# Second graph layer: scores of own frames only, Exp behind the transposes, the routing's tables a step earlier, separate roots

## The chip, the cores and the metric

The kernel runs on one core of one Trainium2 chip. The metric is the device time of one execution in microseconds (us), smaller is better. A measurement of this kernel consists of several runs.

## What is computed

The reference is a stack of two layers over 128 frames of 64 nodes with 128 channels each; a layer is a graph part and a feed-forward part with experts, each added to its input. The change touches the graph part of the second layer and the routing that follows it:

```
def _L1_gnn_ref(inp, adj, W1, W2, W3):
    h1, h2, h3 = inp @ W1, inp @ W2, inp @ W3            # per node
    e = leaky_relu(h1 . h2 within the frame, 0.2)         # 64 x 64 per frame
    e = where(adj > 0, e, NEG_INF)
    return relu(softmax(e) @ h3)
x = x + _L1_gnn_ref(_layernorm(x), adj, W1, W2, W3)
x = x + _L1_ffn_ref(_layernorm(x), Wg, bg, W1, b1, W2, b2)   # top 2 of 8 experts by x @ Wg + bg
```

The second line's experts are computed in a last stage. Before it each token's normalized row has to be written twice into lists in DRAM, one list for each expert, at a position that a running count gives.

## The kernel before, in words

Four phases follow one another: the first graph layer with attention and routing, the first experts, the second graph layer with its routing (`phase_gnn1`, L2357 on), and the last experts (`phase_last`, L2762 on). Only `phase_gnn1` and its class `SplitRouting` (L1230 on) change. All names below are of these two.

The tokens lie in SBUF as 64 pairs of frames: 128 partitions are the 2 x 64 nodes of a pair. Four pairs are a group, and 16 groups are worked on one after another in a software pipeline that is written out by hand: `in_pairs` calls each engine's own `step(g, ...)` for g = -3 to 20, and inside it each piece names the group it works on. Engines meet by semaphores: `x.now(i)` waits for the piece of group i, `x.before(i)` for that of the group in front.

The pieces of a group, in the order in which its data pass them:
- `head_x` on DVE (L2354) adds the first experts' two rows to x; `head_stats` (L280 to L286) takes mean and variance; `roots` on POOL (L2720) takes the reciprocal root by a power; `head_xn` on DVE (L2629) normalizes.
- `head_T` on PE (L2450) transposes the four pairs, ScalarE (ACT) copies them out (L2541), `head_h` (L2458, L2459, L2462) forms h1, h2 and h3, and ACT copies these (L2545, L2552).
- `scores` on PE (L2472, L2475) writes the mask and adds h1 . h2 for whole pairs, 128 x 128 each, of which the two 64 x 64 blocks on the diagonal are used. `scores_own` on ACT (L2572) copies the two blocks out, `soft` on DVE (L2638 to L2645) applies the leaky slope, takes the row maximum and subtracts it. `exp` on ACT (L2581) writes the exponentials into `pr`, whose other blocks were set to zero once (L2418).
- `probs_T` on PE (L2484) transposes `pr`, ACT copies (L2588), `mix` on PE (L2496) multiplies 128 rows of the transposed probabilities with h3 and a column of ones, `norm` on DVE (L2655) takes the reciprocal of the sums, `mixed_out` on ACT (L2563) scales and clips, `residual` on DVE (L2662) adds to x.
- For the routing, `flat_stats` (L280 to L286) and the same `roots` instruction on POOL give a second normalizing, `flat_norm` (L2676) writes the rows, `flat_T` on PE (L2507) transposes them, ACT copies (L2595), `logits` on PE (L1269) multiplies with the routing's matrix.
- Batches of eight pairs (the first two and the last two have four) are then routed: `vector_choose` on DVE (L1304 to L1332) finds the two best experts, `tensor_rank` on PE (L1283, L1286) counts, `vector_rows` on DVE (L1348 to L1357) turns counts into row positions, and `pool_scatter` (L1384) has POOL issue two indirect DMAs for each pair, 128 in all. At most three are under way (`OUT`): each waits for the landing of the third one before it. Position tiles and the three `flat` tiles are used again once their scatters have landed.

The order of the steps is what the change rewrites. Before, in step g the routing's normalizing, transposes and logits belong to group g - 1, and a batch is chosen when `batch_due(g, 3)` holds, that is two steps after its last group. One `roots` instruction in each step serves the head of group g + 2 and the routing of group g - 1. POOL issues up to 16 scatters of a batch in three parts (6, 8 and 2) over three steps, each part behind that step's `roots`:

```
2723                def step(g, b, h):
2724                    roots(g)
2725                    t, u, v = [batch_due(g, lag) for lag in (3, 4, 5)]
```

SP's queue fetches the first experts' rows (L2345, as `head_x` frees a buffer), loads the last stage's weights (L2743) and stores x (L2739). After the last batch's positions DVE builds the last stage's tables (L1443 on), SP writes padding rows behind each list (L1484), waits for the last scatters, and gathers the first rows (L1507).

Of the kernel before, what the change touches and what calls it, by code (L numbers as in the profile page):

```python
# [21 lines left out]
PG = 4  # L22
# [1207 lines left out]
class SplitRouting:  # L1230
# [3 lines left out]
    def __init__(self, ctx, nc, name, consts, base, bias):  # L1234
# [16 lines left out]
        self.pos = [sb(f"pos{i}", [128, 2, PB], I32) for i in range(2)]  # L1251
# [89 lines left out]
    def vector_rows(self, dve, t, bank):  # L1341
# [14 lines left out]
        self.wait_landed(dve, t - 2)  # L1356
        dve.tensor_copy(self.pos[t % 2][:, :, 0:n], self.posf[:, :, 0:n]).then_inc(s.sem, 1)  # L1357
# [16 lines left out]
    def pool_scatter(self, pool, t, first, last, flat, dest):  # L1374
# [4 lines left out]
        for n in range(first, last):  # L1379
# [4 lines left out]
            pool.indirect_dma_start(out=dest, out_offset=bass.IndirectOffsetOnAxis(ap=self.pos[t % 2][:, k, p:p + 1], axis=0),  # L1384
# [972 lines left out]
def phase_gnn1(nc, W, x, banks, c, T, rows1, dest, ahead, wall, out_dram, resident, tile_w):  # L2357
# [3 lines left out]
    with ExitStack() as ctx:  # L2361
# [8 lines left out]
        st, mv = sb("st", [128, 2, PG, 6]), sb("mv", [128, 2, PG, 2])  # L2370
# [9 lines left out]
        pr = sb("pr", [128, PG, 2, NODES])  # L2380
        pt = sb("pt", [128, PG, 128])
# [20 lines left out]
        xT_ready, h12_ready, p_ready, pt_ready, fT_ready = sig("xT_ready"), sig("h12_ready", 2), sig("p_ready", 2), sig("pt_ready"), sig("fT_ready")  # L2402
        own_ready = sig("own_ready", 2)
        act_signals = [xT_ready, h12_ready, h3_ready, own_ready, p_ready, pt_ready, o_ready, fT_ready] + R.act_signals
        root_ready = sig("root_ready")
        pool_signals = [root_ready] + R.pool_signals
# [4 lines left out]
        def own(f):  # L2411

            return bE[64 * f:64 * f + 64, :].rearrange("n (p f m) -> n p f m", p=PG, f=2)[:, :, f, :]

        with nc.Block() as block:
            @block.gpsimd
            def _(pool):
                pool.memset(pr[:, :, :, :], 0.0).then_inc(setup, 1)  # L2418
                pool.memset(h3[:, :, C:C + 1], 1.0).then_inc(setup, 1)
                open_signals(pool, pool_signals)  # L2420
# [20 lines left out]
        with nc.Block() as block:  # L2441
            @block.tensor
            def _(pe):
                def head_T(i):
                    if not runs(i):
                        return
                    pe.wait_ge(*fT_ready.before(i, turns=3))
# [5 lines left out]
                def head_h(i):  # L2453
# [7 lines left out]
                    for p in range(PG):  # L2461
                        ins = pe.matmul(bH3[:, 128 * p:128 * p + 128], xT[:, 128 * p:128 * p + 128], w3[:, :],  # L2462
                                        start=(p == 0), stop=True, skip_group_check=True)
                    ins.then_inc(pe_h.sem, 1)

                def scores(i):
                    if not runs(i):
                        return
                    pe.wait_ge(*pt_ready.before(i))
# [607 lines left out]
```

## Time and profile before

| what | value |
|---|---|
| median of 3 runs | 1493.25 us (1490.9 to 1496.06) |
| span of the profiled execution | 1492.9 us |
| time of the profiled execution outside the span | none is given |
| busy: PE, DVE, ACT, POOL | 79%, 69%, 50%, 58% of the span |
| phase of the change, from the page's slices and the timeline | some 912 to 1197 us |

The span is that of one execution under the profiler; the runs are timed without it. A line of a view names engine, line of the kernel, operation, what is written from what with shapes, and a count; a time in brackets is the engine's idle time before it and what ended it. PE is TensorE's products, PEld its weight loads, DVE VectorE, ACT ScalarE, POOL GpSimd, and SP the engine that issues most DMAs. The granted clock is given as a share of TensorE's full clock.

### The profile page before, as it was taken

To read this page: it belongs to the slowest core of one execution; us is meant where nothing else is said; L and a number is where in the kernel's file an instruction comes from. 1 tells how busy PE (TensorE), PEld (TensorE's weight loads), DVE (VectorE), ACT (ScalarE), POOL (GpSimd) and SP (SyncE) were. 2 spreads that over 40 slices of the span, in tenths; PEclk is the share of its full clock that TensorE was granted. 3 is DMA by queue.
4 is the path that set the end of the run, shared out by engine and by line. 5 is a ranking of instruction groups with operands and counts; after the bars stand their busy time and mean duration, and the time that the engine had idled before them with its cause. 6 is when DMAs were issued, how large, how long until landed. Compare 5 with 4: busy or idle time off the path is not lost. (4 is left out here: it accounts for less than half of the span.)

```text
span 1492.9 us, 32014 instructions
## 1 busy us (share of the span) xinstructions
PE 1180.9 (79%) x8595; PEld 1004.2 (67%) x8595; DVE 1029.2 (69%) x3960; ACT 742.6 (50%) x1864; POOL 869.1 (58%) x742
## 2 busy tenths in 40 slices
PE   5888888767888772599999994666775089999996
PEld 3666656557878772488888883545554079989995
DVE  3788888999888874367777765667775435565554
ACT  5777777546676772133333331434443035555553
POOL 3466666552556777344444442245776748887887
PEclk9999999979898995799999997879777579999999
DMA  7300000000000111466666664233421225545553
GB/s 188 54 2 2 2 1 2 2 1 1 30 30 32 39 41 57 141 196 196 196 196 196 196 209 138 84 93 92 122 94 60 78 50 72 71 63 71 71 69 45
DMA packets 126249, 122.53 MB, mean 82 GB/s; under 512 B 16576, under 2 KB 108096, under 8 KB 126128
## 3 DMA queue, kind: packets, MB, share of 16 engines
q1 hardware_dynamic: 92720, 85.65, 20.4%
q0 software_dynamic: 32960, 35.36, 12.0%
q8 instruction: 53, 0.87, 0.3%
q14 instruction: 68, 0.56, 0.1%
q10 hardware_dynamic: 448, 0.10, 0.0%
HBM read 76.71 MB, written 44.34 MB: 81 GB/s over the span
## 5 line engine op out<-in xcount | busy, mean ns | idle before, releaser
L2866 POOL DMA_INDIRECT out<-m_yb,m_dsti x142 | 228.4, 1608 | 64.3 <-DVE m_yb L2966 26.9
L2160 POOL DMA_INDIRECT rows<-m_yb,m_dsti x135 | 129.2, 957 | 169.5 <-DVE m_dsti L2291 147.9
L1384 POOL DMA_INDIRECT dispatch<-g_flat,g1r_pos x128 | 129.4, 1011 | 76.0 <-issue 32.3
L2236 ACT ACTIVATE m_sg<-psum 128x256 f32<-128x256 f32 (+3 forms) x216 | 79.8, 370 | 178.7 <-PE psum L2189 174.8
L1126 POOL DMA_INDIRECT dispatch<-common_v,a1r_pos x128 | 129.3, 1010 | 54.3 <-issue 35.5
L2939 ACT ACTIVATE m_hT<-psum,m_w 128x256 f32<-128x256 f32 (+1 forms) x240 | 92.8, 447 | 100.7 <-PE psum L2893 99.8
L2189 PE MATMUL psum<-m_xT,m_w 128*128 128x256 f32 (+3 forms) x648 | 140.3, 366 | 0.7 <-ACT m_xT L2227 0.7
L2189 PEld LDWEIGHTS psum<-m_xT,m_w 128*128 128x128 f32 (+1 forms) x648 | 106.2, 178 | 18.3 <-ACT m_xT L2227 0.9
L2904 PE MATMUL psum<-m_w,m_hT 128*128 128x128 f32 x848 | 104.7, 275 | 3.1 <-DVE m_yb L2962 3.1
L2893 PE MATMUL psum<-m_xT,m_w 128*128 128x256 f32 (+1 forms) x480 | 104.9, 363 | 1.0 <-issue 0.8
L2904 PEld LDWEIGHTS psum<-m_w,m_hT 128*128 128x128 f32 x848 | 99.4, 192 | 3.7 <-issue 2.8
L2272 DVE TENSOR_TENSOR m_hT<-psum,m_sg 128x256 f32<-128x256 f32 (+3 forms) x216 | 80.1, 402 | 20.6 <-ACT m_sg L2236 18.9
L2893 PEld LDWEIGHTS psum<-m_xT,m_w 128*128 128x128 f32 x480 | 81.8, 195 | 9.7 <-issue 2.0
L2199 PE MATMUL psum<-m_w,m_hT 128*128 128x128 f32 (+1 forms) x606 | 76.6, 274 | 0.5 <-DVE m_yb L2256 0.5
L491 PE MATMUL psum<-ident,common_s 128*128 128x128 f32 x256 | 41.6, 285 | 42.0 <-ACT common_s L635 42.0
L2199 PEld LDWEIGHTS psum<-m_w,m_hT 128*128 128x128 f32 (+1 forms) x606 | 71.9, 191 | 0.8 <-DVE m_hT L2272 0.7
L2759 DVE COPY m_w<-resident 128x1156 f32 x60 | 47.6, 793 | 35.4 <-issue 35.3
L2033 POOL TENSOR_TENSOR a_root<-a_pin,a_cube 128x12 f32<-128x12 f32 (+2 forms) x20 | 38.8, 1941 | 54.1 <-DVE a_pin L1987 50.8
L491 PEld LDWEIGHTS psum<-ident,common_s 128*128 128x128 f32 x256 | 27.9, 142 | 61.0 <-ACT common_s L635 60.8
L2256 DVE TENSOR_TENSOR m_yb<-psum,m_share 128x256 f32<-128x256 f32 (+1 forms) x72 | 29.4, 408 | 56.6 <-PE psum L2199 49.7
L480 PE MATMUL psum<-g_k,g_q 128*128 128x256 f32 x256 | 65.7, 379 | 0.0
L720 DVE TENSOR_REDUCE g_mx<-psum 128x8 f32<-128x512 f32 x64 | 43.9, 686 | 23.4 <-PE psum L480 23.4
(316 smaller groups left out, 3219.4 us busy)
## 6 DMA issues: line engine op xcount, KB each, us to landing
m_w<-in_c_wall SPq DMA_DIRECT2D x54, 533.0 KB
ahead_w<-in_c_wall SPq DMA_DIRECT2D x18, 533.0 KB, 4.2
g1c_y<-rows SPq DMA_DIRECT2D x32, 256.0 KB, 3.4
m_xg<-dispatch SPq DMA_DIRECT2D x47, 132.0 KB
m_xg<-dispatch SPq DMA_DIRECT2D x46, 130.0 KB, 2.2
resident<-in_c_wall SPq DMA_DIRECT2D x8, 578.0 KB, 6.0
out<-x SPq DMA_DIRECT2D x16, 256.0 KB, 5.9
out<-m_yb,m_dsti POOLq DMA_INDIRECT x142, 3.3
```

What stands on the lines that cost most here:

```text
L491: ins = pe.transpose(bPT[:, 128 * hp:128 * hp + 128], s[:, p % 2, 2 * hp:2 * hp + 2, :].rearrange("p h m -> p (h m)"), ident[:, :])
L1126: pool.indirect_dma_start(out=dest, out_offset=bass.IndirectOffsetOnAxis(ap=self.pos[t % 2][:, k, p:p + 1], axis=0), in_=flat[:, p, :], in ...
L1384: pool.indirect_dma_start(out=dest, out_offset=bass.IndirectOffsetOnAxis(ap=self.pos[t % 2][:, k, p:p + 1], axis=0), in_=flat[:, p, :], in ...
L2160: pool.indirect_dma_start(out=rows_out, out_offset=bass.IndirectOffsetOnAxis(ap=dsti[j][:, t:t + 1], axis=0), in_=yb[j][:, t, :], in_offse ...
L2189: i = pe.matmul(bank[0:cn, TILE * m:TILE * m + rows], w[j][:, HID * m + c0:HID * m + c0 + cn], xT[j % 2][:, 0:rows], start=(m == 0), stop= ...
L2199: i = pe.matmul(bY[:, 128 * t:128 * t + 128], hT[jj % 2][0:cn, k, 128 * t:128 * t + 128], w[jj][0:cn, W2 + 128 * k:W2 + 128 * k + 128], st ...
L2236: act.activation(sg[j % 2][0:cn, k, 0:rows], up_banks[j % 2][k][0:cn, 0:rows], ACT.Silu)\
L2272: dve.tensor_tensor(hT[j % 2][0:cn, k, 0:rows], up_banks[j % 2][k][0:cn, TILE:TILE + rows], sg[j % 2][0:cn, k, 0:rows], ALU.mult).then_inc ...
L2866: pool.indirect_dma_start(out=out_rows, out_offset=bass.IndirectOffsetOnAxis(ap=dsti[j][:, t:t + 1], axis=0), in_=yb[j][:, t, :], in_offse ...
L2893: i = pe.matmul(bank[0:cn, TILE * (k % 2):TILE * (k % 2) + rows], w[j][:, c0:c0 + cn], xT[j % 2][:, 0:rows], start=(k % 2 == 0), stop=True ...
L2904: i = pe.matmul(bY[:, 128 * t:128 * t + 128], hT[jj % 2][0:cn, k, 128 * t:128 * t + 128], w[jj][0:cn, HID + 128 * k:HID + 128 * k + 128], ...
L2939: act.activation(hT[j % 2][0:cn, n, 0:rows], bank[0:cn, TILE * (n % 2):TILE * (n % 2) + rows], ACT.Gelu, bias=w[j][:, b1:b1 + 1]).then_inc ...
```

## The change

- Scores: only the blocks of own frames are formed, 64 x 64 each, into one half of a bank (`own`); the mask covers 256 columns in place of 512. ACT copies them once with the factor 0.2, and DVE takes the maximum of that copy and of `own` itself.
- The shifted scores `s` are transposed as two blocks of 128 x 128 (`turned`, the other half of the bank) and Exp is applied when ACT copies the result into `pt`. `pr`, its memset, `exp` and `p_ready` go.
- `mix` works on 64 rows and 64 columns at a time: eight products in place of four, whose input rows and output partitions take either half of the array. h3 is formed in eight products, so that its rows lie where these need them.
- Order: each engine's step g now begins with the transposes of the shifted scores of group g, which the step before has made, and ends with `flat_norm`, `flat_T` and `logits` of group g itself. A batch is chosen when `batch_due(g, 2)` holds, one step after its last group. `scores` and `soft` are those of group g + 1.
- `roots` becomes `root_head(g + 2)` and `root_flat(g)`, each an instruction of its own on four columns, with scatters between them. A batch's 16 scatters come in parts of 3, 4, 4 and 5.
- A third position tile; `mv` is split, with two tiles for the heads.

The core of the diff:

```diff
-        self.pos = [sb(f"pos{i}", [128, 2, PB], I32) for i in range(2)]
+        self.pos = [sb(f"pos{i}", [128, 2, PB], I32) for i in range(3)]
...
-        self.wait_landed(dve, t - 2)
-        dve.tensor_copy(self.pos[t % 2][:, :, 0:n], self.posf[:, :, 0:n]).then_inc(s.sem, 1)
+        self.wait_landed(dve, t - 3)
+        dve.tensor_copy(self.pos[t % 3][:, :, 0:n], self.posf[:, :, 0:n]).then_inc(s.sem, 1)
...
-        def own(f):
-
-            return bE[64 * f:64 * f + 64, :].rearrange("n (p f m) -> n p f m", p=PG, f=2)[:, :, f, :]
+        own, turned = bE[:, 0:256], bE[:, 256:512]
...
+                    for f in range(2):
+                        for p in range(PG):
+                            r, n = 64 * (p % 2), 2 * (p // 2) + f
+                            ins = pe.matmul(bH3[r:r + 64, 128 * n:128 * n + 128], xT[:, 128 * p + 64 * f:128 * p + 64 * f + 64], w3[:, :],
+                                            start=(f == 0 and p < 2), stop=True, skip_group_check=True)
+                    ins.then_inc(pe_h.sem, 1)
...
+                    pe.wait_ge(*e_steps.before(i, 0))
+                    pe.wait_ge(*h12_ready.now(i, 1))
+                    mk = bass.AP(mask, 0, [mask[:, :].ap[0], [0, PG], [1, NODES]])
+                    pe.matmul(own, identb[:, :], mk, start=True, stop=False, skip_group_check=True)
                     for p in range(PG):
-                        ins = pe.matmul(bH3[:, 128 * p:128 * p + 128], xT[:, 128 * p:128 * p + 128], w3[:, :],
-                                        start=(p == 0), stop=True, skip_group_check=True)
-                    ins.then_inc(pe_h.sem, 1)
-
-                def scores(i):
+                        for f in range(2):
+                            t = slice(128 * p + 64 * f, 128 * p + 64 * f + 64)
+                            ins = pe.matmul(own[64 * f:64 * f + 64, 64 * p:64 * p + 64], h1[:, t], h2[:, t], start=False, stop=True,
+                                            skip_group_check=True)
+                    ins.then_inc(pe_e.sem, 1)
...
-                    pe.wait_ge(*h12_ready.now(i, 1))
-                    mk = bass.AP(mask, 0, [mask[:, :].ap[0], [0, 2 * PG], [1, NODES]])
-                    pe.matmul(bE[:, :], identb[:, :], mk, start=True, stop=False, skip_group_check=True)
-                    for p in range(PG):
-                        t = slice(128 * p, 128 * p + 128)
-                        ins = pe.matmul(bE[:, t], h1[:, t], h2[:, t], start=False, stop=True, skip_group_check=True)
-                    ins.then_inc(pe_e.sem, 1)
-
...
-                    pe.wait_ge(*p_ready.now(i, 1))
-                    for p in range(PG):
-                        ins = pe.transpose(bE[:, 128 * p:128 * p + 128], pr[:, p, :, :].rearrange("n f m -> n (f m)"), ident[:, :])
+                    pe.wait_ge(*e_steps.now(i, 2))
+                    for q in range(2):
+                        ins = pe.transpose(turned[:, 128 * q:128 * q + 128], s[:, 2 * q:2 * q + 2, :].rearrange("n p m -> n (p m)"), ident[:, :])
...
-                    for u, bank in enumerate([bO0, bO1]):
-                        for n in range(2):
-                            p = 2 * u + n
-                            ins = pe.matmul(bank[:, (C + 1) * n:(C + 1) * n + C + 1], pt[:, p, :], h3[:, p, :],
-                                            start=(n == 0), stop=True, skip_group_check=True)
-                        ins.then_inc(pe_o.sem, 1)
+                    for u in range(2):
+                        for n, bank in enumerate([bO0, bO1]):
+                            for f in range(2):
+                                r = slice(64 * n, 64 * n + 64)
+                                ins = pe.matmul(bank[64 * f:64 * f + 64, (C + 1) * u:(C + 1) * u + C + 1], pt[r, u, 64 * f:64 * f + 64],
+                                                h3[r, 2 * u + f, :], start=(u == 0), stop=True, skip_group_check=True)
+                            if u == 1:
+                                ins.then_inc(pe_o.sem, 1)
...
                 def step(g, b, h):
-                    scores(g)
+                    probs_T(g)
                     head_T(g + 1)
+                    mix(g)
                     head_h(g + 1)
-                    probs_T(g)
-                    if b % 2 == 1:
-                        mix(g)
-                    t = batch_due(g, 3)
+                    scores(g + 1)
+                    t = batch_due(g, 2)
                     if t is not None:
                         R.tensor_rank(pe, t, bR)
-                    flat_T(g - 1)
-                    if b % 2 == 0:
-                        mix(g)
-                    logits(g - 1)
+                    flat_T(g)
+                    logits(g)
...
-                    for f in range(2):
-                        r = slice(64 * f, 64 * f + 64)
-                        act.activation(e0[r, :, :], own(f), ACT.Copy).then_inc(own_ready.sem, 1)
...
-                    for f in range(2):
-                        r = slice(64 * f, 64 * f + 64)
-                        act.activation(pr[r, :, f, :], s[r, :, :], ACT.Exp).then_inc(p_ready.sem, 1)
+                    act.activation(e0[:, :, :].rearrange("n p m -> n (p m)"), own, ACT.Copy, scale=0.2).then_inc(own_ready.sem, 1)
...
-                    act.activation(pt[:, :, :].rearrange("m p n -> m (p n)"), bE[:, :], ACT.Copy).then_inc(pt_ready.sem, 1)
+                    act.activation(pt[:, :, :].rearrange("m q n -> m (q n)"), turned, ACT.Exp).then_inc(pt_ready.sem, 1)
...
                 def step(g, b, h):
-                    scores_own(g)
+                    probs_T(g)
+                    head_xT(g + 1)
+                    mixed_out(g)
                     head(g + 1)
-                    exp(g)
-                    probs_T(g)
-                    t = batch_due(g, 3)
+                    scores_own(g + 1)
+                    head_h3(g + 1)
+                    t = batch_due(g, 2)
                     if t is not None:
                         R.scalar_exp(act, t, batch_rows(flat, t))
-                    flat_T(g - 1)
-                    mixed_out(g)
-                    head_h3(g + 1)
+                    flat_T(g)
...
-                    dve.wait_ge(*own_ready.now(i, 1))
+                    dve.wait_ge(*own_ready.now(i))
                     dve.wait_ge(*e_steps.before(i))
-                    dve.scalar_tensor_tensor(out=e1[:, :, :], in0=e0[:, :, :], scalar=0.2, in1=e0[:, :, :],
-                                             op0=ALU.mult, op1=ALU.max).then_inc(e_steps.sem, 1)
+                    dve.tensor_tensor(e1[:, :, :], own.rearrange("n (p m) -> n p m", p=PG), e0[:, :, :], ALU.max).then_inc(e_steps.sem, 1)
...
-                               vs[1], i, EPS_LN, gate, [x3_ready.now(i)] + ([root_ready.now(i + 2)] if i > 0 else []))
+                    norm_stats(dve, lambda p: xt(i, p), st[:, 1, :, :], mv1, ve[:, 1, :], bn[1], part[1],
+                               vs[1], i, EPS_LN, gate, [x3_ready.now(i), rs1_ready.before(i)])
...
-                    dve.wait_ge(*root_ready.now(i + 3))
+                    dve.wait_ge(*rs1_ready.now(i))
...
                 def step(g, b, h):
-                    flat_stats(g - 1)
-                    soft(g)
-                    t = batch_due(g, 3)
+                    t = batch_due(g, 2)
+                    norm(g)
+                    head_x(g + 3, 1 - b % 2)
                     if t is not None:
                         R.vector_choose(dve, t, bR)
-                    if b % 2 == 1:
-                        flat_norm(g - 1, h)
-                        norm(g)
-                        if t is not None:
-                            R.vector_rows(dve, t, bR)
-                        head_x(g + 3, 1 - b % 2)
-                        head_xn(g + 2)
                     else:
-                        if t is not None:
-                            R.vector_rows(dve, t, bR)
-                        head_x(g + 3, 1 - b % 2)
-                        flat_norm(g - 1, h - 1)
-                        head_xn(g + 2)
-                        norm(g)
-                    head_stats(g + 3)
+                        head_stats(g + 3)
                     residual(g)
+                    flat_stats(g)
+                    soft(g + 1)
+                    if t is not None:
+                        R.vector_rows(dve, t, bR)
+                    head_xn(g + 2)
+                    flat_norm(g, h)
+                    if t is not None:
+                        head_stats(g + 3)
...
-                def roots(g):
...
-                    pool.tensor_tensor(rs[:, lo:hi, :], ve[:, lo:hi, :], half[:, 0:PB].rearrange("t (k p) -> t k p", k=2)[:, lo:hi, :],
-                                       ALU.pow).then_inc(root_ready.sem, 1)
+                def root_head(i):
+                    if not runs(i):
+                        return
+                    pool.wait_ge(*vs[0].now(i))
+                    pool.wait_ge(*xn_ready.before(i))
+                    pool.tensor_tensor(rs[:, 0, :], ve[:, 0, :], half[:, 0:PG], ALU.pow).then_inc(rs0_ready.sem, 1)
...
+                def root_flat(i):
+                    if not runs(i):
+                        return
+                    pool.wait_ge(*vs[1].now(i))
+                    pool.wait_ge(*flat_ready.before(i))
+                    pool.tensor_tensor(rs[:, 1, :], ve[:, 1, :], half[:, 0:PG], ALU.pow).then_inc(rs1_ready.sem, 1)
...
+                def some(t, first, last):
+                    if t is not None and BATCHES[t][1] == PB:
+                        R.pool_scatter(pool, t, first, last, batch_rows(flat, t), dest)
 
                 def step(g, b, h):
-                    roots(g)
-                    t, u, v = [batch_due(g, lag) for lag in (3, 4, 5)]
-                    if v is not None and BATCHES[v][1] == PB and v < LAST_BATCH - 2:
-                        R.pool_scatter(pool, v, 14, 16, batch_rows(flat, v), dest)
-                    if u is not None and BATCHES[u][1] == PB:
-                        R.pool_scatter(pool, u, FIRST_PART if u == LAST_BATCH - 2 else 6, 14 if u < LAST_BATCH - 2 else 16, batch_rows(flat, u), dest)
-                    if t is not None:
-                                R.pool_scatter(pool, t, 0, 2 * PG if BATCHES[t][1] == PG else FIRST_PART if t == LAST_BATCH - 2 else 6, batch_rows(flat, t), dest)
+                    t, u, v = [batch_due(g, lag) for lag in (2, 3, 4)]
+                    root_head(g + 2)
+                    if v != LAST_BATCH - 2:
+                        some(v, 11, 16)
+                    some(u, 3, 7)
+                    root_flat(g)
+                    some(u, 7, 11 if u != LAST_BATCH - 2 else 16)
+                    some(t, 0, 3)
+                    if t is not None and BATCHES[t][1] == PG:
+                        R.pool_scatter(pool, t, 0, 2 * PG, batch_rows(flat, t), dest)
```

## Rows read from the trace of the kernel before

**Rows 1.** One line's instructions, L1384: ns min/median/max, first and last start in us.
```profile
L1384 POOL DMA_INDIRECT dispatch<-g_flat,g1r_pos x128: 952/958/1485, 963.1 to 1194.0; - x128
```

**Rows 2.** Groups of POOL by line and shape, 912 to 1197 us: busy, mean ns, idle before.
```profile
L1384 POOL DMA_INDIRECT dispatch<-g_flat,g1r_pos x128 | 129.4, 1011 | 76.0 <-issue 32.3 <-DVE g1r_pos L1357 26.4 <-DMA dispatch<-g_flat,g1r_pos 17.0
...
L2720 POOL TENSOR_TENSOR g_rs<-g_ve,half 128x4 f32<-128x4 f32 x6 | 6.9, 1154 | 14.3 <-DVE g_ve L286 14.2
```

**Rows 3.** Timeline (start us, us, engine, line): last positions, first gather of the last stage.
```profile
1174.85 0.17 DVE L1357 CAST g1r_pos<-g1r_posf 128x8 int32<-128x8 f32 x1 [6.20 <-DMA dispatch<-g_flat,g1r_pos]
...
1196.55 0.41 SPq L1507 DMA_DIRECT2D ahead_xg<-dispatch  x1
```

**Rows 4.** Timeline of DVE, one choosing and one unbroken run, 1006 to 1021 us.
```profile
1006.06 0.21 DVE L1304 TENSOR_TENSOR g1r_lg<-psum,W_bg 128x64 f32<-128x64 f32 x1
...
1009.11 1.11 DVE L2676 TENSOR_SCALAR g_flat<-x,g_mv,g_rs 128x128 f32<-128x128 f32 x4
...
1011.87 0.31 DVE L1348 TENSOR_TENSOR g1r_rows<-psum,stab_base 128x144 f32<-128x144 f32 x1 [0.16 <-PE psum L1286]
...
1013.02 1.41 DVE L2354 TENSOR_TENSOR x<-x,g1c_y 128x512 f32<-128x512 f32 x2
...
1014.35 1.11 DVE L2629 TENSOR_SCALAR g_xn<-x,g_mv,g_rs 128x128 f32<-128x128 f32 x4
...
1015.37 0.86 DVE L280 BATCH_NORM_STATS2 g_st<-x 128x6 f32<-128x128 f32 x4
...
1016.87 0.68 DVE L2662 TENSOR_TENSOR x<-x,g_o 128x512 f32<-128x512 f32 x1
...
1020.51 1.44 DVE L2354 TENSOR_TENSOR x<-x,g1c_y 128x512 f32<-128x512 f32 x2
```

**Rows 5.** Busy time by stretch: sum of PE, PEld, DVE, ACT, POOL, then granted clock.
```profile
1005.00:1024.00 19.00, 11.71 (x74) 8.40 (x74) 14.50 (x58) 9.31 (x22) 9.67 (x8) 1.00 0.21 62
...
1069.00:1079.00 10.00, 8.54 (x29) 6.13 (x29) 8.89 (x34) 4.07 (x10) 7.59 (x8) 0.50 0.32 99
```

**Rows 6.** Timeline, PE and DVE, at the lower clock.
```profile
1068.78 1.09 PE L2507 MATMUL psum<-ident,g_flat 128*128 128x128 f32 x4 [3.78 <-DVE g_flat L2676]
...
1072.27 0.59 PE L2472 MATMUL psum<-g_mask,identb 128*128 128x512 bf16 x1
...
1145.92 1.09 PE L2484 MATMUL psum<-ident,g_pr 128*128 128x128 f32 x4 [3.22 <-ACT g_pr L2581]
...
1147.74 2.06 PE L2496 MATMUL psum<-g_h,g_pt 128*128 128x129 f32 x8 [0.73 <-issue]
...
1149.84 0.17 DVE L2655 RECIPROCAL g_rc<-psum 128x2 f32<-128x2 f32 x1 [0.69 <-PE psum L2496]
```

**Rows 7.** Timeline of PE at the upper clock.
```profile
1010.37 1.13 PE L2496 MATMUL psum<-g_h,g_pt 128*128 128x129 f32 x8 [0.73 <-issue]
...
1011.69 0.64 PE L2507 MATMUL psum<-ident,g_flat 128*128 128x128 f32 x4
...
1013.92 0.38 PE L2472 MATMUL psum<-g_mask,identb 128*128 128x512 bf16 x1
```

**Rows 8.** Timeline of PE, two more transposes after a wait.
```profile
964.70 1.08 PE L2507 MATMUL psum<-ident,g_flat 128*128 128x128 f32 x4 [3.57 <-DVE g_flat L2676]
...
1136.92 0.63 PE L2507 MATMUL psum<-ident,g_flat 128*128 128x128 f32 x4 [3.13 <-DVE g_flat L2676]
```

**Rows 9.** Timeline of PE and PEld in the first layer, 200 to 212 us.
```profile
201.69 1.08 PE L453 MATMUL psum<-g_xT,g_wqkv 128*64 128x256 f32 x8
...
208.16 1.03 PE L480 MATMUL psum<-g_k,g_q 128*128 128x256 f32 x4
...
201.69 0.63 PEld L453 LDWEIGHTS psum<-g_xT,g_wqkv 128*64 128x64 f32 x8 [0.17 <-issue]
```

**Rows 10.** Timeline, first scores and the load of Exp's table.
```profile
930.33 1.05 PE L2475 MATMUL psum<-g_h 128*128 128x128 f32 x8
...
935.58 1.28 ACT L2581 ACT_TABLE_LOAD   x1
```

More of the change, by code:

```diff
@@ L2369, in phase_gnn1 @@
         mask = sb("mask", [128, NODES], BF16)
-        st, mv = sb("st", [128, 2, PG, 6]), sb("mv", [128, 2, PG, 2])
+        st = sb("st", [128, 2, PG, 6])
+        mv0, mv1 = [sb(f"mv0{i}", [128, PG, 2]) for i in range(2)], sb("mv1", [128, PG, 2])
         ve, rs = sb("ve", [128, 2, PG]), sb("rs", [128, 2, PG])
@@ L2379, in phase_gnn1 @@
         s = sb("s", [128, PG, NODES])
[L2380 to L2381 removed]
+        pt = sb("pt", [128, 2, 128])
         rc = sb("rc", [128, PG])
@@ L2446, in head_T @@
                         return
-                    pe.wait_ge(*fT_ready.before(i, turns=3))
+                    pe.wait_ge(*fT_ready.before(i, turns=2))
                     pe.wait_ge(*xn_ready.now(i, PG - 1))
@@ L2502, in flat_T @@
                         return
-                    if runs(i + 2):
-                        pe.wait_ge(*xT_ready.now(i + 2))
+                    if runs(i + 1):
+                        pe.wait_ge(*xT_ready.now(i + 1))
                     pe.wait_ge(*flat_ready.now(i, PG - 1))
@@ L2535, in _, with head_xT @@
             def _(act):
-                def head(i):
+                def head_xT(i):
                     if not runs(i):
@@ L2541, in head @@
                     act.activation(xT[:, :], bT[:, :], ACT.Copy).then_inc(xT_ready.sem, 1)
+                def head(i):
+                    if not runs(i):
+                        return
                     for n, (bank, h) in enumerate([(bH1, h1), (bH2, h2)]):
@@ L2556, in mixed_out @@
                         return
-                    for u, bank in enumerate([bO0, bO1]):
-                        act.wait_ge(*rc_ready.now(i, u))
+                    for n, bank in enumerate([bO0, bO1]):
+                        act.wait_ge(*rc_ready.now(i, n))
                         act.wait_ge(*x3_ready.before(i))
                         ov = bank[:, 0:2 * (C + 1)].rearrange("n (p c) -> n p c", p=2)
-                        for n in range(2):
-                            p = 2 * u + n
-                            act.activation(o[:, p, :], ov[:, n, 0:C], ACT.Relu, scale=rc[:, p:p + 1]).then_inc(o_ready.sem, 1)
+                        for u in range(2):
+                            act.activation(o[:, 2 * u + n, :], ov[:, u, 0:C], ACT.Relu, scale=rc[:, 2 * n + u:2 * n + u + 1]).then_inc(o_ready.sem, 1)
                 def scores_own(i):
@@ L2619, in head_stats @@
                         return
-                    norm_stats(dve, lambda p: xt(i, p), st[:, 0, :, :], mv[:, 0, :, :], ve[:, 0, :], bn[0], part[0],
-                               vs[0], i, EPS_LN, gate, [M.mixed.now(i, 1), root_ready.before(i)])
+                    norm_stats(dve, lambda p: xt(i, p), st[:, 0, :, :], mv0[i % 2], ve[:, 0, :], bn[0], part[0],
+                               vs[0], i, EPS_LN, gate, [M.mixed.now(i, 1), rs0_ready.before(i)])
                 def head_xn(i):
@@ L2642, in soft @@
                     dve.wait_ge(*e_steps.now(i, 1))
-                    dve.wait_ge(*p_ready.before(i))
+                    dve.wait_ge(*pe_pt.before(i))
                     m = mx[:, :]
```

37 lines of the change are left out of this document (11 added, 26 removed).

## Prediction

> **What bounds the kernel now.** I first read the page's 40 slices to find the stage that the change touches: the second graph layer with its routing lies between the two expert stages. Then I listed all instructions of GpSimd (POOL) in it. Its 128 scatters start between 963.1 and 1194.0 us [rows 1], each takes 0.96 us, and some 0.30 us of issue (32.3 us over 109) lies before the next [rows 1, 2]; so one costs 1.26 us of POOL. The last ends at 1194.96 us, and 1.6 us later SP gathers the first rows of the last stage [rows 3]. That stage works through a fixed list of tiles, so the whole kernel ends later or sooner by what this gather moves. 128 scatters are 161 us of a stretch of 232 us; the rest are roots, waits for positions (26.4 us) and waits for landings (17.0 us) [rows 2]. So POOL ends the stage, with one batch of work after another, and the question is when the last batches reach it. Next I read the timeline of VectorE (DVE) for the price of every piece of a step [rows 4], and that of TensorE at its two clock levels [rows 5 to 8].
>
> **The new loop.** Afterwards a step on DVE begins with the reciprocals of group g, which wait for the mixing products, and ends with the normalizing into the routing's rows, on which the transposes of the same group wait. Those are followed on TensorE, in its queue's order, by the logits, by the transposes of the next group's scores and by its mixing, and only then DVE has work again (but for a statistics piece in routing steps). No step can overlap the next there. A step is therefore DVE's pieces plus one **turn** through TensorE and ScalarE, which I call L.
>
> DVE's pieces, from start to start [rows 4]: routing's rows 1.15 us (1011.87 to 1013.02), adding the experts' rows 1.33, normalizing for the next head 1.02, first statistics 1.50 (1015.37 to 1016.87), residual with second statistics and softmax 3.64 (to 1020.51), choosing 3.05 (1006.06 to 1009.11), normalizing for the routing 1.11, and 0.17 for the second reciprocal. A plain step holds 0.17 + 1.33 + 1.50 + 3.64 + 1.02 + 1.11 = 8.77 us. A routing step has choosing and rows in addition, and its statistics go behind the last piece, into the turn: 11.47 us. The half batches I take as full ones; that is some tenths too much.
>
> The turn at the lower clock: flat's transposes to the instruction behind the logits 3.49 us (1068.78 to 1072.27); the scores' transposes to the second reciprocal 3.92 us (1145.92 to 1149.84) [rows 6]. From the latter goes about 0.4, since two transposes of the four remain (their 1.09 us is at most halved), and about 0.2 for an Exp over 256 columns where a copy over 512 stood; I take 0.4 us for that Exp, and leave the mixing as it is. Added is 0.17 us of idle weight load where full blocks give way to half ones [rows 9], once on this path. Sum 7.0 us. At the upper level the first part is 2.23 us (1011.69 to 1013.92), and the second loses 2.06 - 1.13 = 0.93 of mixing and 0.23 of transposes [rows 6, 7]: 2.2 + 2.1 + 0.2 = 4.5 us.
>
> **The mixing blocks.** Four products of 128 rows become eight of 64 by 64. Upper bound among likely prices: two half-wide blocks share the array, so the mixing costs what it costs now. The trace shows just that for column halves: eight instructions of 128 by 64 over 256 columns took 1.08 us, four of full width 1.03 [rows 9]. Lower bound: blocks that differ in rows share it too, and the mixing is halved, which takes 1.0 us from the turn at the lower clock and 0.55 at the upper (6.0 and 4.0 us). No row reaches that; I take the middle, 6.5 and 4.25 us; the two ends are rivals below.
>
> **The clock.** The granted clock was 1.00 from 1005 to 1024 us and 0.50 from 1069 to 1079 us, its two levels of 2.4 and 1.2 GHz [rows 5]. Four transposes take 0.63 us at the one and 1.09 at the other. Of four resumptions after TensorE had waited between 3.1 and 3.8 us, three were at the lower level (964.70, 1068.78, 1145.92) and one at the upper (1136.92) [rows 6, 8]. Afterwards TensorE has nothing to do from the end of the scores to flat's transposes, while DVE does most of its pieces, that is for a good part of its 8.8 to 11.5 us in each step, and so at least as long as in those four waits. So I take the lower level for three turns in four: L = 0.75 x 6.5 + 0.25 x 4.25 = 5.9 us.
>
> **The sum.** The first scores come as now (930.33 us [rows 10]), then 0.7 for them, 0.4 for the copy, 1.2 for the softmax, 0.5 for two transposes, 1.28 for the load of Exp's table [rows 10], 0.4 for Exp, 1.2 for mixing: step 0 begins at 936 us. Before step 14 lie seven plain and seven routing steps: 7 x 8.77 + 7 x 11.47 = 141.7, less 2.8 us at group 13, which has no more head to add and measure. Step 14 starts at 1074.9 + 14 L. It has 9.1 us on DVE (11.47 less 1.33 and 1.02), so step 15 starts at 1084.0 + 15 L. Its second statistics are done after 0.17 + 3.05 + 2.4 = 5.6 us. The root for them stands in POOL's queue ahead of 25 scatters (nine of batch 7, eight each of 8 and 9): 0.2 + 1.15 for the root [rows 2] and 25 x 1.26 = 31.5 us. The last scatter ends at 1122.5 + 15 L = 1211 us. Now it is 1195.0, so the stage ends 16 us later. Break-even is L = 4.83 us.
>
> What lies beside this: SP's path from the last positions to the gather is 21.7 us now (1174.85 to 1196.55 [rows 3]); afterwards step 15's pieces (7.9) end at 1084 + 88.5 + 7.9 = 1180.4, the first part of a turn, choosing, counting and rows (3.5 + 3.05 + 0.5 + 1.15) bring the positions at 1188.6, and the gather could go at 1210, 2 us ahead of the scatters' landing. The third position buffer removes the 6.20 us wait of that row; without it POOL would still end last. Narrower scores, one copy of own blocks in place of two, and third products in half blocks cost and save nothing, as DVE's pieces cover them; without that cover they are worth under 1 us in a step. Single roots (32 for 19) need 1.15 us each on POOL [rows 2], which has 16 x 1.26 + 4 x 1.4 = 25.8 us of work in a pair of steps of 8.77 + 11.47 + 2 L = 32 us; so POOL idles in mid-stage, and its landing waits (17.0 us in all now) mostly vanish in that room. DMAs and SP's queue keep their number and order. Routing a step sooner brings the first scatter to 936 + 8.77 + 5.9 + 9.3 = 960 us, 3 us sooner than 963.1: the longer steps in front take back what the shift gives.
>
> The profiled execution spans 1492.9 us, 0.35 below the median of the runs shown, 1493.25; no time outside the span is given. 1492.9 + 16 = **1509 us**.
>
> **Rivals.**
> - Faster: TensorE keeps its upper level through the turns. For it speaks the resumption at 1136.92 [rows 8]; against it, the three others. Then L is 4.0 to 4.5, the last scatter ends at 1182.5 to 1190, and the time is 1480 to 1488 us. It decides as soon as L falls below 4.83.
> - No change: some 70 turns in 100 at the upper level, L from 4.55 to 5.1, 1488.4 to 1497.4 us.
> - Four blocks share the array: L = 0.75 x 6.0 + 0.25 x 4.0 = 5.5, the end at 1205, 1503 us. Only pairs share it: L = 0.75 x 7.0 + 0.25 x 4.5 = 6.4, 1516 us. The Trainium skill (TensorEngine Tiling (Array Packing), Tiling Modes) has four 64x64 tiles work independently; by that rule it is the former. The same section says that changing the tiling mode drains the engine, which speaks against this change; the trace agrees with a small price, the 0.17 us of rows 9.
> - Much slower: half blocks run one at a time, the mixing doubles, and L is about 8.2: 1543 us. Rows 9 speak against it, for columns at least. Further waits (own scores late for the softmax, a root behind scatters that wait for landings) would stop on the way there.
> - The earlier routing does what it says and POOL, started sooner, ends the stage sooner. For that POOL would have to be the bound throughout, and its 25.8 us in a pair of steps against at least 20.2 + 2 x 4.0 speak against it. That the routing hardly starts sooner at all (the 3 us above) is part of every case here.
>
> **How the numbers follow.** A measurement of this kernel can tell about 0.3%, 4.5 us. The forecast with L from 5.2 to 7.1 (1498 to 1527 us) gets 0.61; in it, 0.25 are for sharing by four, 0.20 for pairs alone, 0.16 between them. The much slower rivals get 0.10, the faster one 0.15, no change 0.14. So slower is 0.71. The forecast's own range is 1498 to 1527. The range for all, 1486 to 1527, takes in no change and the upper edge of the faster rival, and leaves out some 0.1 on each side.
>
> **What would show it.** DVE should idle before its reciprocals, waiting for the mixing, by some 4 to 7 us in each of 16 steps. Between 930 and 1170 us the granted clock should be lower than 0.8. Pairs of steps should last about 32 us; under 29.7 the forecast of the sign is wrong. POOL's wait for the second statistics should replace its waits for positions, and the last scatter should end near 1211 us. The mixing's group shows whether four blocks share the array. If flat's transposes resume at 0.63 us in most steps, my clock is wrong; if DVE's pieces overlap the turn, my loop is.

## The result and the profile after

The changed kernel took 1527.35 us (median of 4 runs, 1523.85 to 1527.66) against 1494.24 us before (4 runs, 1490.9 to 1496.06): 1.0221 times as long, 95% interval 1.0203 to 1.0239. It is slower, as forecast, but by 33 us where 16 were forecast, and 1527.35 lies 0.35 us above the range.

The profiled execution after spans 1525.7 us; its run took 1527.64 us, so 1.9 us lie outside the span. These are the scatters' line and the groups of POOL from 925 to 1240 us, which answer to [rows 1, 2]:

```profile
L1384 POOL DMA_INDIRECT dispatch<-g_flat,g1r_pos x128: 954/958/1442, 967.6 to 1228.7; - x128
...
L1384 POOL DMA_INDIRECT dispatch<-g_flat,g1r_pos x128 | 128.4, 1003 | 53.6 <-issue 35.6 <-DVE g1r_pos L1357 17.6 <-DVE g1r_posf L1354 0.3
L2700 POOL TENSOR_TENSOR g_rs<-g_ve,half 128x4 f32<-128x4 f32 x16 | 17.3, 1079 | 25.8 <-DVE g_xn L2621 16.7 <-DVE g_ve L286 8.9
L2707 POOL TENSOR_TENSOR g_rs<-g_ve,half 128x4 f32<-128x4 f32 x16 | 16.5, 1030 | 72.9 <-DVE g_ve L286 72.9
```

The first scatter went 4.5 us later than before and the last 34.7 us later. No scatter waits for a landing any more (17.0 us before), the waits for positions fell from 26.4 to 17.6 us, and POOL now stands 72.9 us in front of its second roots, waiting for DVE's statistics: POOL idles in mid-stage. The waits of DVE and PE from 925 to 1230 us (total, times, longest, in us) and the busy times from 930 to 1170 us, with the granted clock behind them, show for whom:

```profile
DVE g_rc L2646 <- PE psum L2498: 84.1, 16, 6.3
...
PE psum L2510 <- DVE g_flat L2667: 84.4, 16, 6.8
```

```profile
930.00:1170.00 240.00, 151.19 (x1078) 100.19 (x1078) 140.84 (x607) 71.59 (x174) 120.81 (x119) 0.70 0.28 83
```

DVE waits for the mixing and PE for DVE's rows, 84 us each, 16 times, in turn: DVE's pieces and the way through PE and ACT don't overlap, but for the statistics in routing steps. The granted clock is 0.70; it was 0.79 in the same stretch before. One whole turn, as the prediction calls that way, at the end of a routing step, in the timeline:

```profile
1054.65 0.87 DVE L280 BATCH_NORM_STATS2 g_st<-x 128x6 f32<-128x128 f32 x4
1054.88 1.09 PE L2510 MATMUL psum<-ident,g_flat 128*128 128x128 f32 x4 [6.40 <-DVE g_flat L2667]
...
1056.01 0.60 ACT L2587 ACTIVATE g_fT<-psum 128x512 f32<-128x512 f32 x1 [6.84 <-PE psum L2510]
...
1056.66 1.87 PE L1269 MATMUL psum<-W_wg,g_fT 128*128 128x8 f32 x8 [0.69 <-ACT g_fT L2587]
...
1058.38 0.67 PE L2485 MATMUL psum<-ident,g_s 128*128 128x128 f32 x2
...
1059.09 0.38 ACT L2580 ACTIVATE g_pt<-psum 128x256 f32<-128x256 f32 x1 [2.48 <-PE psum L2485]
...
1059.83 1.14 PE L2498 MATMUL psum<-g_h,g_pt 64*64 64x129 f32 x16
...
1061.01 0.26 DVE L2646 RECIPROCAL g_rc<-psum 128x2 f32<-128x2 f32 x2 [4.76 <-PE psum L2498]
```

From the end of the routing's normalizing (1053.88 + 0.85 = 1054.73) to the reciprocals is 6.27 us. In a routing step 1.5 us of it hold the statistics, and 4.76 us are idle; in a plain step all 6.27 are. The end of the stage, which answers to [rows 3]:

```profile
1205.35 0.22 DVE L1357 CAST g1r_pos<-g1r_posf 128x8 int32<-128x8 f32 x1
...
1228.66 0.96 POOL L1384 DMA_INDIRECT dispatch<-g_flat,g1r_pos  x1 [0.30 <-issue]
...
1231.25 0.41 SPq L1507 DMA_DIRECT2D ahead_xg<-dispatch  x1
```

The gather goes 34.7 us later than in [rows 3]. The experts' last rows before the stage were already 3.1 us later in this execution (909.6 against 906.5 us), in code that the change doesn't touch, and the last stage was 1.9 us shorter. So the stage itself is 31.6 us longer.

### The profile page after: what moved, and what is told of

Read it like the earlier page. It is cut to its first block and busy times, and to the rows that moved or that the text cites. A ratio compares the mean times of both kernels' runs of the same rounds, so it can differ in the third digit from the quotient of the medians.

```text
span 1525.7 us, 32671 instructions
## 1 busy us (share of the span) xinstructions
PE 1191.4 (78%) x8947; PEld 995.9 (65%) x8947; DVE 1026.1 (67%) x3960; ACT 719.5 (47%) x1816; POOL 872.2 (57%) x754
## 5 line engine op out<-in xcount | busy, mean ns | idle before, releaser
L1384 POOL DMA_INDIRECT dispatch<-g_flat,g1r_pos x128 | 128.4, 1003 | 53.6 <-issue 35.6
L2510 PE MATMUL psum<-ident,g_flat 128*128 128x128 f32 x64 | 15.9, 398 | 84.4 <-DVE g_flat L2667 84.4
L491 PE MATMUL psum<-ident,common_s 128*128 128x128 f32 x256 | 41.6, 286 | 41.8 <-ACT common_s L635 41.8
L491 PEld LDWEIGHTS psum<-ident,common_s 128*128 128x128 f32 x256 | 27.9, 142 | 60.8 <-ACT common_s L635 60.6
L2510 PEld LDWEIGHTS psum<-ident,g_flat 128*128 128x128 f32 x64 | 10.5, 201 | 85.8 <-issue 81.2
```

Source lines behind the costliest of these rows:

```text
L491: ins = pe.transpose(bPT[:, 128 * hp:128 * hp + 128], s[:, p % 2, 2 * hp:2 * hp + 2, :].rearrange("p h m -> p (h m)"), ident[:, :])
```

## The experiments

Seven kernels, compared with the kernel before on the same chip. In the profiles of all of them the experts' last rows start between 906.9 and 914.8 us, so stages are compared from that row on: to the gather it takes 290.0 us before and 321.6 us after.

**The new blocks in the old order.** The kernel before, with the scores', transposes', Exp's, mixing's and third products' pieces of the changed kernel and nothing else:

```diff
-                    act.activation(pt[:, :, :].rearrange("m p n -> m (p n)"), bE[:, :], ACT.Copy).then_inc(pt_ready.sem, 1)
+                    act.activation(pt[:, :, :].rearrange("m q n -> m (q n)"), turned, ACT.Exp).then_inc(pt_ready.sem, 1)
...
                     head(g + 1)
-                    exp(g)
                     probs_T(g)
```

> The change's blocks alone (own-frame scores, one copy, two wide transposes and then Exp, 64-row mixing and third products), in the order of work of the kernel before, with its joint roots, its routing three steps behind and its two position buffers. Theory (the new order costs the time, the blocks save a little): PE and ACT have less to do, POOL still ends the stage; last scatter between 1180 and 1196 us where it was 1194.0, time 1478 to 1497 us. Rival (half-size products, their changes of shape and the Exp behind the transposes cost it): 1505 to 1527 us.

Measured: 1486.58 us (8 runs), 0.9919 of before (0.9896 to 0.9941). The scatters' line of it:

```profile
L1384 POOL DMA_INDIRECT dispatch<-g_flat,g1r_pos x128: 956/962/1484, 960.9 to 1185.6; - x128
...
  issue: 40.1, 109
  DMA dispatch<-g_flat,g1r_pos: 17.7, 10
  DVE g1r_pos L1357: 11.4, 7
```

The blocks save 0.8%. With 1.0221 for the whole change, the rest of it (the order, with its single roots, scatter parts and third position tile; from here on "the order") costs 1.0221 / 0.9919 = 1.030, some 45 us. The stage takes 279.1 us, 42.5 less than in the changed kernel. Positions come sooner (11.4 us of waits for them, 26.4 before), which fits the shorter work on PE and ACT, and POOL's last scatter still ends the stage. The granted clock is hardly higher than in the changed kernel (0.71 from 930 to 1170 us, against 0.70): a low clock alone doesn't make the stage long.

**Flat's transposes and logits behind the next mixing.** The changed kernel with these on PE and ACT a step later, and routing with them:

```diff
-                    t = batch_due(g, 2)
+                    t = batch_due(g, 3)
...
-                    flat_T(g)
-                    logits(g)
+                    flat_T(g - 1)
+                    logits(g - 1)
```

> The changed kernel, with flat's transposes and logits of group g moved on PE and ACT behind the mixing of group g + 1, and routing a step later with them (three steps behind, as in the kernel before). Blocks, separate roots, DVE's order and three position buffers stay. Theory (a step is long because flat's transposes and logits stand between DVE's last piece and the next mixing): DVE's idle before the reciprocals falls from 4.8 to 6.3 us to under 4 us a step, a pair of steps from 33.0 to about 27 us; the later routing gives back one step of 13 us at the start; time 1470 to 1495 us. Rival (PE's and DVE's work itself is longer, or POOL is the bound): 1515 to 1535 us.

Measured: 1494.03 us (10 runs), 0.9976 of before (0.995 to 1.0002). Of the order's 45 us, (1.0221 - 0.9976) x 1494 = 37 are gone, and the stage takes 284.3 us, 37.3 less than in the changed kernel. DVE's reciprocals of a pair of steps show it, and what ends the pairs now:

```profile
1053.97 0.28 DVE L2646 RECIPROCAL g_rc<-psum 128x2 f32<-128x2 f32 x2
...
1056.86 0.87 DVE L280 BATCH_NORM_STATS2 g_st<-x 128x6 f32<-128x128 f32 x4 [1.30 <-POOL g_rs L2700]
...
1065.95 1.28 DVE L2667 TENSOR_SCALAR g_flat<-x,g_mv,g_rs 128x128 f32<-128x128 f32 x4 [2.83 <-POOL g_rs L2707]
1066.98 0.25 DVE L2646 RECIPROCAL g_rc<-psum 128x2 f32<-128x2 f32 x2
...
1079.79 1.28 DVE L2667 TENSOR_SCALAR g_flat<-x,g_mv,g_rs 128x128 f32<-128x128 f32 x4 [2.26 <-POOL g_rs L2707]
...
1082.33 0.28 DVE L2646 RECIPROCAL g_rc<-psum 128x2 f32<-128x2 f32 x2
```

The pair lasts 28.4 us (33.0 in the changed kernel), and its reciprocals wait for nothing; in the whole stage they wait 5.5 us where it was 84.1. In place of the mixing DVE waits for POOL's roots, 41.6 us in the stage (11.1 of them at once, for a head's root in step 4), and POOL has landing waits again (16.3 us). So the turn is off the path, and the waits now point to POOL; the last experiment tests that. The 8 us of the order that remain are not divided further: no kernel here has the new order with joint roots.

**Idle transposes in TensorE's wait.** The changed kernel with:

```diff
+WARM = (22, 36)
...
+                    for _ in range(WARM[batch_due(i, 2) is not None]):
+                        pe.transpose(bT[:, 0:128], ident[:, :], ident[:, :])
                     pe.wait_ge(*flat_ready.now(i, PG - 1))
```

> The changed kernel, with idle transposes of the identity (22 in a plain step, 36 in a routing step, into the bank that flat's transposes then overwrite) put into TensorE's wait for the normalized rows. Theory (the turn is 6.26 us because TensorE resumes at 1.2 GHz after its wait): the granted clock between 930 and 1170 us rises from 0.70 to over 0.9, the turn falls to 4.0 to 4.4 us, 16 turns give 30 to 36 us, time 1490 to 1498 us. Rival (what TensorE does in that wait doesn't set the clock of the turn): the idle transposes at 0.27 us each end after the rows are ready, by 1.8 us in a plain and 3.4 us in a routing step, and the time is 1550 to 1570 us.

Measured: 1508.17 us (10 runs), 1.0067 of before (1.0033 to 1.0101). The stage takes 304.0 us, 17.6 less than in the changed kernel, by the ratios it is 23 us less: between the theory and the rival. The granted clock from 930 to 1170 us rose to 0.82, not over 0.9. Idle transposes and the turn behind them, in TensorE's timeline:

```profile
1043.69 4.13 PE L2510 MATMUL psum<-ident 128*128 128x128 f32 x36
...
1049.38 0.66 PE L2513 MATMUL psum<-ident,g_flat 128*128 128x128 f32 x4 [1.57 <-DVE g_flat L2670]
1050.72 1.12 PE L1270 MATMUL psum<-W_wg,g_fT 128*128 128x8 f32 x8 [0.69 <-ACT g_fT L2590]
1051.69 0.67 PE L2486 MATMUL psum<-ident,g_s 128*128 128x128 f32 x2
...
1053.14 1.14 PE L2499 MATMUL psum<-g_h,g_pt 64*64 64x129 f32 x16
```

Flat's transposes now ran at the upper level in 14 turns of 16 (0.60 to 0.66 us). But the clock fell again inside the turn: here the logits took 1.12 us, near the 1.06 of the upper level (1.87 at the lower), but the scores' transposes and the mixing took the 0.67 and 1.14 us of the lower one. Only two of the 15 mixings behind a turn kept the upper level's 0.67 us from end to end. A turn wholly at the upper level, before the reciprocals at 1037.89 us, left DVE idle for 3.94 us, against 6.27 at the lower. So the clock does make the turn longer, and filling the wait in front of it isn't enough to hold it.

**Flat's transposes three times over.**

```diff
-                    for p in range(PG):
+                    for p in list(range(PG)) * 3:
```

> The changed kernel, with flat's four transposes done three times over into the same places: eight transposes more in each turn, 0.27 us each at the lower clock. Theory (nothing overlaps the turn, so the stage pays for each microsecond in it 16 times): 8 x 0.27 = 2.2 us a turn, 35 us in all; time 1552 to 1565 us (less, down to 1540 us, if the longer burst brings the clock up before the logits). Rival (POOL bounds the stage, steps have room): 1525 to 1533 us.

Measured: 1539.51 us (4 runs), 1.0298 of before (1.0241 to 1.0356): 12 us more than the changed kernel (8.5 in the stage), just under the theory's lower case and above the rival's range. The two ratios' intervals (from 1.0241 here, to 1.0239 there) only just part, so I go by the waits: DVE's before its reciprocals are 96.9 us in all, for 84.1. Two turns, and PE's busy time and the granted clock during the first one's transposes:

```profile
1037.10 2.79 PE L2510 MATMUL psum<-ident,g_flat 128*128 128x128 f32 x12 [4.87 <-DVE g_flat L2667]
1042.30 0.67 PE L2485 MATMUL psum<-ident,g_s 128*128 128x128 f32 x2
...
1056.51 2.79 PE L2510 MATMUL psum<-ident,g_flat 128*128 128x128 f32 x12 [6.50 <-DVE g_flat L2667]
1060.91 0.41 PE L2485 MATMUL psum<-ident,g_s 128*128 128x128 f32 x2
...
1061.84 0.67 PE L2498 MATMUL psum<-g_h,g_pt 64*64 64x129 f32 x16
```

```profile
1037.10:1039.90 2.80, 2.79 (x12) 0.50 0.14 48
```

The eight transposes more take 2.79 - 1.09 = 1.70 us, 0.21 each and not 0.27, though the granted clock was 0.50 throughout: the 0.27 was 1.09 / 4, and the 1.09 holds, by this estimate, 1.09 - 4 x 0.21 = 0.25 us that a burst pays once. In turns like the first the rest stays at the lower level too, and DVE's idle grows from 6.27 to 7.97 us, the whole 1.70. In turns like the second (seven of the 15 that a mixing follows, five of them in routing steps) the rest runs at the upper level and gives it all back (4.67 us of idle before the reciprocals at 973.56, for 4.76 in the changed kernel). So what is put into the turn is paid in full, unless the rest of the turn gets the upper level with it.

**Two position buffers.** The changed kernel with:

```diff
-        self.pos = [sb(f"pos{i}", [128, 2, PB], I32) for i in range(3)]
+        self.pos = [sb(f"pos{i}", [128, 2, PB], I32) for i in range(2)]
...
-        self.wait_landed(dve, t - 3)
+        self.wait_landed(dve, t - 2)
```

> The changed kernel with two position buffers in place of three. Theory (in the new order the scatters have no backlog when positions are due, except in the last batches, where POOL works through 25 scatters in a row whatever the positions do): no wait for the landing of older rows before the conversion to positions in mid-stage, one of up to 6 us at the end that nothing waits for; time within 4 us of the changed kernel, 1523 to 1531 us. Rival (the third buffer carries the new order): 1533 us or more.

Measured: 1529.6 us (2 runs), 1.0224 of before (1.0179 to 1.027). From the first reciprocals to those of step 15 it takes 247.8 us, as in the changed kernel, the stage takes 321.2 us, and one wait for landings of 3.7 us appears, at the end, which nothing waits for. As far as two runs and a profile can tell, the third buffer does nothing here.

**Six scatters in flight.** Two kernels with

```diff
-OUT = 3
+OUT = 6
```

the first on the new blocks in the old order (and with three position tiles), the second on the kernel with flat's transposes a step later.

> The new blocks in the order of the kernel before (as in the first experiment, 1486.6 us), with six scatters in flight instead of three in both layers and three position buffers. Theory (in that order POOL sets the pace: 16 scatters, two joint roots and one wait of some 4 us for a landing make the 28.8 us of a pair): the landing waits (17.7 us in all) mostly go, a pair lasts 25 to 27 us, time 1466 to 1480 us. Rival (PE and DVE set the pace, POOL's waits are slack): 1483 to 1490 us.

> The changed kernel with flat's transposes and logits, and routing, a step later (as in the second experiment, 1494.0 us), with six scatters in flight instead of three in both layers. Theory (once the turn is off DVE's path POOL sets the pace, 28.4 us a pair, of it 3 to 4 us landing wait): pairs of 25 to 27 us, time 1474 to 1487 us. Rival (DVE and PE set the pace): 1490 to 1498 us.

Measured: 1483.17 us (4 runs), 0.9913 of before (0.9881 to 0.9946), and 1480.73 us (4 runs), 0.9898 (0.9861 to 0.9934); the stages take 275.4 and 269.7 us. The waits behind the scatters' lines, of the first and then of the second:

```profile
L1384 POOL DMA_INDIRECT dispatch<-g_flat,g1r_pos x128: 952/958/1481, 960.3 to 1181.8; - x128
...
  DVE g1r_pos L1357: 30.8, 8
```

```profile
L1384 POOL DMA_INDIRECT dispatch<-g_flat,g1r_pos x128: 954/958/1415, 971.8 to 1178.6; - x128
...
  DVE g1r_pos L1357: 4.5, 3
```

In both the landing waits are gone. In the old order waits for positions took their place (30.8 us where 11.4 were), and the time is the same within what can be told: there the rival holds, though the pairs of steps 6 to 11, which took between 27.9 and 28.9 us, take 27.2 to 27.5. In the new order with flat's work a step later nothing took their place. A pair lasts 25.4 us, near the 25.2 us that 16 scatters at 1.26 and four roots at 1.25 us need, so POOL works without a pause and sets the pace. That kernel has the lowest median of all, but its ratio can't be told from that of the first of the two.

## Where the prediction held and where it failed

**The loop: right.** DVE's pieces and the turn alternate, and nothing overlaps but the statistics, as forecast: 84.1 us of idle in 16 waits. Steady plain steps last 15.3 us and routing steps 17.7 us; 8.77 + 6.27 = 15.04 and 11.47 + 6.27 = 17.74 by the prediction's pieces. Moving the first part of the turn away took 37 us back, and 1.70 us put into it came out as 1.70 us of idle where the clock stayed the same, which shows it.

**The mixing blocks: the lower bound holds.** 1.14 us at the lower clock against 2.06 [rows 6], so four blocks share the array, and the middle that I took was 0.5 us too dear. By the Trainium skill (TensorEngine Tiling (Array Packing), Tiling Modes) four 64x64 tiles work independently; the trace agrees. That alone, with the rest as forecast, gave the rival's 1503 us, so other steps failed the other way.

**The clock: the first step that failed.** "So I take the lower level for three turns in four" treated a turn as being at one level from end to end. For flat's transposes the share was nearly right: 3 of 16 were at the upper level, and one was in part. But the logits behind them and the mixings were at the lower in all 16. Where the transposes had the upper level, the clock fell inside the turn:

```profile
1037.63 0.63 PE L2510 MATMUL psum<-ident,g_flat 128*128 128x128 f32 x4 [4.14 <-DVE g_flat L2667]
1038.94 1.87 PE L1269 MATMUL psum<-W_wg,g_fT 128*128 128x8 f32 x8 [0.69 <-ACT g_fT L2587]
...
1042.12 1.14 PE L2498 MATMUL psum<-g_h,g_pt 64*64 64x129 f32 x16
```

This is one of the three, from the changed kernel, and even it gives back only 0.46 us. The trace of the kernel before showed the same. The one resumption at the upper level that I counted, at 1136.92 us [rows 8], went on like this:

```profile
1137.39 1.66 PE L2496 MATMUL psum<-g_h,g_pt 128*128 128x129 f32 x8
1138.84 1.71 PE L1269 MATMUL psum<-W_wg,g_fT 128*128 128x8 f32 x8
```

That is 1.66 us of mixing, for 1.13 at the upper level [rows 7], and logits at a granted clock of 0.50. And two more waits for flat's rows, of 6.55 us before 997.50 and of 3.08 us before 1025.34, which I had left out, ended at the lower level (1.08 and 1.09 us).

So L was 6.19 us on the average of steps 0 to 13 and not 5.9. A turn wholly at the lower level took 6.27 us, where my pieces give 6.0 with four blocks sharing; the other 0.27 are 0.15 from DVE's end to the transposes, for which I had no term, and 0.12 in the second part, from which I took too much away; in it the idle weight load in front of the mixing, for one, was 0.33 us for the 0.17 of my sum. Against 5.5, the value of my own rival for four blocks, the error is 0.7 us a turn, 10 us in all. By luck the middle value for the blocks hid over half of it.

**The terms beside the turn: the second step that failed.** "The first scores come as now", "less 2.8 us at group 13" and roots that cost no wait were terms that I left as they were or took off without looking at what stood behind them; the figures are of the profiled execution. The first reciprocals came at 941.99 us for 936: 3.1 us of that are the late start of this execution, and 2.7 of the other 2.9 are in the first scores. In the run-in DVE now puts the second group's statistics ahead of the first head's normalizing, so that the first head's transposes come 1.6 us later; the rest is lost behind them at the lower clock, most of it in the third products (1.98 us, 1.28 before). From there to step 14 it took 232.6 us for 221.5. The turn has 0.29 x 14 = 4.1 us of this. Step 13 has 2.4: where there is no more head to add and measure, I took 2.8 us off, but waits came to light that this work had covered, of 1.12 us for the clipped products and 1.05 us for the copied scores. Step 3 has 2.6: its statistics waited 2.56 us for a root behind scatters on POOL, a cost of single roots that I had set to nothing. The remaining 2.0 us are spread over the others. Step 14 and the tail cost 1.5 us more, and the last stage was 1.9 us shorter. Together 3.1 + 2.9 + 11.1 + 1.5 - 1.9 = 16.7 us, which is 1525.7 less 1509. Of it the turn has 4.1, the terms beside it 11.4, and this execution's start and end 1.2.

**The rivals.** Faster and no change fell with the clock. Pairs alone sharing the array named 1516 us, nearer than mine, for a reason that the mixing's 1.14 us rules out. Half blocks one at a time fell with the same number; the further waits named beside them did come, but small (2.56 us for a root behind scatters that waited for no landing, 1.05 for own scores). POOL as the bound throughout fell for this order with its 72.9 us in front of the second roots.

**The tail and POOL: right.** The last scatter ended 39.8 us behind step 15's reciprocals (38.5 forecast), and the gather 1.6 us after it, as before. That two position tiles would do was right. That POOL has room in mid-stage was right for this order and those close to it; with flat's work a step later POOL sets the pace. **Earlier routing: right in kind.** It starts no scatter sooner: 967.6 us less 3.1 is 964.5, for 963.1 before, where I had forecast 960.

**The range** ended at L = 7.1, and the turn stayed well inside. The forecast of 16 us was short by half, and the range was left, by the 12.6 us beside the turn, for which the sum had no term: a run-in that was read as unchanged, covers that go with the work they covered, a wait for a single root, and an execution that begins its stage 3 us later. The range was left by only 0.35 us, and its base was a span: the span after, 1525.7 us, lies inside it. The size was wrong all the same, 33 us for 16.

## What to carry to other kernels

When a reordering ties an engine's last piece of a step to its first piece of the next, through another engine's queue, count the whole way round as a serial turn, and if it consists of short products with waits between, price it at the slow clock for its whole length: in the changed kernel the logits and the mixing ran there in 16 turns of 16, whatever level the first transposes had. Price blocks and order apart: here the blocks were worth 0.8% and the order cost 3%. Moving two pieces one step later took most of that back, and with more scatters in flight the kernel was 1% faster than before (0.9898), which can't be told from the blocks in the old order with as many (0.9913). Where work is left out in the last rounds, look for what it used to cover before you take its time off.

## What was not expected of the hardware

- TensorE's clock fell from the upper to the lower level within a turn, behind 4.13 us of unbroken idle transposes, a pause of 1.57 us, 0.66 us of transposes and a pause of 0.69 us. In that kernel the idle transposes brought flat's transposes to the upper level in 14 turns of 16, the logits behind them wholly in seven, and the mixing behind those wholly in two of 15.
- Twelve transposes after a wait took 2.79 us whether the wait had lasted 4.87 or 6.50 us, at a granted clock of 0.50. Each further transpose of a burst costs 0.21 us at the lower level (1.70 / 8), less than the 0.27 that a quarter of the 1.09 us of four suggests, so a burst is not priced by its mean.
- Step lengths repeat very closely: the kernels with two and with three position tiles both took 247.8 us for 15 steps, while the start of the stage differed by 2.7 us between their executions.
